# Products that nobody reads, put between TensorE's waits and among the lead's maxima, and one early exponential, in a hybrid block with attention

## What is computed

```
x = x + mix(layernorm(x))          # gate * fuse(causal conv path, symmetric conv path), projections, residual
x = x + ffn(layernorm(x))          # 128 -> 512, relu squared, 512 -> 128, ternary weights and a low-rank part
x = x + attention(layernorm(x))    # 16 heads of size 8
x = x + ffn(layernorm(x))

# attention; B=2 sequences, S=1024 tokens
qkv    = x @ qkv_w.T + qkv_b
scores = q.T k / sqrt(8)
w      = softmax(scores)           # over the keys
out    = (w v) @ out_w.T + out_b
```

## Time and profile before

| | us |
|---|---|
| median of 3 runs | 528.9 (528.67 to 528.9) |
| profiled execution, its own time | 530.41 |
| span of the profiled execution | 528.6 |
| PE busy | 498.6 (94%) |
| DVE busy | 438.3 (83%) |
| ACT busy | 358.3 (68%) |
| POOL busy | 70.2 (13%) |

### The profile page before, as it was taken

The page is one execution under the profiler, slowest core; times in us unless marked ns, Lnnn a source line. Parts: engine busy times, 40 slices in busy tenths (PEclk is TensorE's granted clock), DMA queues, the critical chain, the costliest instruction groups (busy, mean ns, idle before and its releaser), DMA issues.

```text
span 528.6 us, 10281 instructions
## 1 busy us (share of the span) xinstructions
PE 498.6 (94%) x4118; PEld 228.3 (43%) x4118; DVE 438.3 (83%) x654; ACT 358.3 (68%) x691; POOL 70.2 (13%) x89
## 2 busy tenths in 40 slices
PE   4999999998799999999999999999999999998897
PEld 2454566765333333333333333333333333332576
DVE  5699149948897999999999999999999999921953
ACT  2726214354117888888888888888888888888431
POOL 4399930000010001001001000000000000000000
PEclk9999999999757999999999999999999999999899
DMA  8100000053400202003002002101100000000001
GB/s 209 42 2 2 1 9 1 1 208 110 151 10 1 70 15 81 2 2 82 2 1 75 11 1 53 31 1 42 42 2 2 2 2 3 1 1 2 0 21 60
DMA packets 14110, 17.96 MB, mean 34 GB/s; under 512 B 3600, under 2 KB 10175, under 8 KB 13551
## 3 DMA queue, kind: packets, MB, share of 16 engines
q1 hardware_dynamic: 13036, 16.58, 10.7%
q0 software_dynamic: 240, 0.46, 0.5%
q10 hardware_dynamic: 786, 0.27, 0.2%
HBM read 11.70 MB, written 5.24 MB: 32 GB/s over the span
## 4 chain that ended last, share of the span: by engine, by line
PE 82%; DVE 8%; ACT 5%; DMA 2%; issue 1%; SPq 1%; ACTq 0%; DVEq 0%
PE ps L1344 31%; PE ps L1395 26%; PE ps L1137 6%; PE ps L1127 6%; DVE mx L995 4%; PE ps L1148 2%; ACT gate L739 2%; PE ps L1362 2%; PE ps L1173 1%; PE ps L1159 1%; PE ps L1184 1%; PE ps L1114 1%; PE ps L1320 1%; ACT acc L739 1%; DMA x<-in_L_attn_a_x 1%
## 5 line engine op out<-in xcount | busy, mean ns | idle before, releaser
L995 DVE TENSOR_REDUCE mx<-ps 128x1 f32<-128x1024 f32 x256 | 312.8, 1225 | 15.9 <-PE ps L1344 13.8
L1344 PE MATMUL ps<-kt,qt 62*128 62x512 f32 x512 | 195.1, 464 | 7.1 <-DVE mx L995 4.1
L1362 PE MATMUL ps<-qt,kt 64*128 64x512 f32 x512 | 184.3, 452 | 0.8 <-ACT gate L739 0.7
L739 ACT ACTIVATE acc<-ps 128x512 f32<-128x512 f32 x256 | 138.6, 603 | 26.6 <-PE ps L1362 21.8
L739 ACT ACTIVATE gate<-ps 128x512 f32<-128x512 f32 x256 | 138.5, 604 | 15.7 <-PE ps L1362 12.7
L1344 PEld LDWEIGHTS ps<-kt,qt 62*128 62x128 f32 x512 | 80.0, 193 | 110.2 <-DVE mx L995 79.1
L1395 PE MATMUL ps<-gate,val 128*32 128x256 f32 (+1 forms) x976 | 81.4, 405 | 3.8 <-ACT gate L739 3.8
L1395 PE MATMUL ps<-acc,val 128*32 128x256 f32 (+1 forms) x976 | 80.5, 402 | 0.9 <-ACT acc L739 0.9
L1362 PEld LDWEIGHTS ps<-qt,kt 64*128 64x128 f32 x512 | 75.8, 186 | 12.5 <-ACT gate L739 6.4
L498 POOL TENSOR_TENSOR nm_s<-nm,nm_s 16x128 f32<-16x128 f32 x16 | 7.6, 477 | 266.3 <-ACT nm L717 266.3
L1395 PEld LDWEIGHTS ps<-gate,val 128*32 128x32 f32 x976 | 19.3, 108 | 47.2 <-issue 23.5
(11 more groups left out here) (182 smaller groups left out, 369.3 us busy)
## 6 DMA issues: line engine op xcount, KB each, us to landing
qt<-q_scr SPq DMA_DIRECT2D x64, 64.0 KB
kt<-k_scr SPq DMA_DIRECT2D x32, 128.0 KB
x<-in_L_attn_a_x SPq DMA_DIRECT2D x4, 256.0 KB, 5.6
q_scr<-attn SPq DMA_DIRECT2D x4, 256.0 KB, 2.2
k_scr<-attn SPq DMA_DIRECT2D x4, 256.0 KB, 2.4
q_scr<-gate SPq DMA_DIRECT2D x4, 256.0 KB, 2.1
k_scr<-gate SPq DMA_DIRECT2D x4, 256.0 KB, 2.3
qt<-nm_s SPq DMA_DIRECT2D x64, 4.0 KB
```

The costliest lines, as they stand in the source:

```text
L739: act.activation(pexp[step % NPB][:, j, :], bank(e_bank(slot)), ACT.Exp, scale=SCALE).then_inc(e_read, 1)
L995: dve.tensor_reduce(mx[:, item % 2, at:at + 1], pair(lo), AX.X, ALU.max).then_inc(m_read, 1)
L1344: mm = pe.matmul(bank(m_banks(M_UNIT[u])[keys]), qt[r][rows, half, jj, c * P:(c + 1) * P], kt[r][rows, jj, keys, :], start=True, stop=True)
L1362: pe.matmul(bank(e_bank(slot)), kt[r][rows, jj, s // TC, s % TC * P:(s % TC + 1) * P], qt[r][rows, half, jj, :], start=True, stop=True).th ...
```

## The change

A helper `keep_busy(b, n, cols)` on PE issues n float32 products of `ident` with the first `cols` columns of `ident` into PSUM bank b; nothing reads them, they wait for nothing and count no semaphore. Seven of 128 columns stand behind the wait for `ident_ready`, ahead of that for `in_w`, and eight behind the transposes of `in_w`, ahead of the wait for `s_w_fold`; they write bank 5, which nothing uses yet (`IDLE_BANK`). In the lead, two of 96 columns follow each of the units 6 to 21, into bank 2, which is free there. On ACT one exponential of 128x1, of a column of `ident` into a new tile `warm`, stands right behind `negate(0)`.

```
--- before.py
+++ after.py
@@ -60,6 +60,7 @@
 
 EBANKS = (0, 1, 3)
 O_BANK = 2
+IDLE_BANK = 5
 MBANKS = ((4, 5), (6, 7))
 HT = QH * TC
 NU = NI * HT
@@ -254,6 +255,7 @@
         mixed_q = [acc[:, r // 2, 1, r % 2 * CH:(r % 2 + 1) * CH] for r in range(4)]
         mx = sb("mx", [P, 2, HT])
         nm = sb("nm", [HT, P])
+        warm = sb("warm", [P, 1])
         nm_s = sb("nm_s", [HT, PARTS, P])
 
         ps = [ctx.enter_context(nc.psum_tensor(f"ps{i}", [P, 2 * CH], F32)) for i in range(4)]
@@ -723,6 +725,7 @@
                 act.activation(o_sb[:, :], bank(O_BANK), ACT.Copy).then_inc(o_copied, 1)
 
             negate(0)
+            act.activation(warm[:, :], ident[:, 0:1], ACT.Exp)
             for i in range(2):
                 act.wait_ge(scr_done[i], 2 * STORED)
             for hn in range(NI):
@@ -1095,11 +1098,18 @@
         @block.tensor
         def _(pe):
 
+            def keep_busy(b, n, cols):
+
+                for _ in range(n):
+                    pe.matmul(bank(b)[:, 0:cols], ident[:, :], ident[:, 0:cols], start=True, stop=True)
+
             pe.wait_ge(ident_ready, 1)
+            keep_busy(IDLE_BANK, 7, P)
             pe.wait_ge(s_w_in, 16)
             for m in range(4):
                 mm = pe.transpose(bank(1)[:, m * P:(m + 1) * P], in_n[:, m, :], ident[:, :])
             mm.then_inc(setup_mm, 1)
+            keep_busy(IDLE_BANK, 8, P)
             pe.wait_ge(s_w_fold, 16 * 3)
             for i, src in enumerate((hb_n, ha_n)):
                 for k in range(KC):
@@ -1457,6 +1467,7 @@
                 if u == TURN_FIRST_AT:
                     turn_max(0)
                 unit(u)
+                keep_busy(O_BANK, 2, P * 3 // 4)
             for hn in range(NI):
                 n, half = divmod(hn, 2)
                 pe.wait_ge(shift_in, (hn + 1) * SHIFT)
```

## The result

The changed kernel takes 544.04 us in the median of four runs (541.58 to 545.2), against 528.9 for the kernel before: ratio 1.0258, 95% interval 1.0229 to 1.0288. That is 15 us slower. It is the side of the rival *Slower*, for which 538 had been worked out at a chance of 0.05. The profiled execution took 545.2 us with a span of 543.4.

The account below looks back on a forecast made before the run. PE was taken to bound the attention loop, slowed by a low clock. Setup 2.0 plus lead, table and slow half steps 5.2 made 7.2 us off 530.41: 523.2, or 521.7 as the runs' median; range 520.4 to 525.5.

Parts of the forecast that it names:

- Slower: Rival, chance 0.05: lead fillers never raise the clock, each of 15 periods takes 1.98 instead of 1.265 us; total 538.
- Part 1: First loads: setup products raise the clock early, so the run of products starting at 15.96 us comes 2.0 us sooner.
- So it is kept: Setup: the 2.0 us stay won, since evacuations, table load and copy follow from it, then PE works without a break.
- The rule of the Trainium skill weighed there: Setup rival, chance 0.25: transposes neither raise nor hold the clock, so only 0.45 us is gained there; total 523.2.
- Part 2: Lead, units 6 to 21: clock holds, products are hidden, maxima stand 1.14 us apart instead of 1.265; 2.0 us won.
- one fall: Rival, chance 0.15: clock falls at the lead's head, two units at 1.98 us, 1.7 us back; total 523.4 or 524.9.
- The price of a unit's two products: Lead: two 96-column products cost 0.45 us per unit at full clock and 0.85 at the low one.
- the cover that the prediction called thin: Lead at full clock: PE occupied 0.57 + 0.45 = 1.02 of each 1.14 us, products hidden with 0.1 us over.
- the decision point: Lead: the kernel turns slower where the filler at the low clock costs more than 0.14 us per unit.
- Part 3 and the loop's start: Early exponential and attention loop's start: fifth half step's products with v come 5.2 us earlier, lead and table included.
- The table load: ACT's load before the loop's first exponential moves into idle time near 151 us; 1.3 us won.
- The end: Kernel's tail: the clock's fall at 492.8 us may move, vanish or last longer; +-1 us, taken as 0.

Follow-up runs that it names:

- e1: Changed kernel with only the fifteen setup products kept; 529.07 us median of ten, against 530.27 for the kernel before, ratio 0.9987.
- e4: Changed kernel without setup products, plus seven 128-column products ahead of unit 6; 526.15 to 528.15 us in five executions, 532.22, 532.83 and 545.3 in the others.
- e9: e8 plus one product of 512 columns over 64 rows per lead unit; 526.11 us median of ten, ratio 0.9947 to the kernel before.
- e10: e9 plus the fifteen setup products and eight of 128 columns in front of unit 0; 524.13 us median of four, ratio 0.99.
- e11: e10 plus three 128-column products behind the last product with v and five behind the last transpose of o; 524.39 us median of four, ratio 0.9902.
- e3: Changed kernel with only the early exponential kept; 530.44 us median of ten, against 530.27 for the kernel before.
- e7: Changed kernel with each lead unit's two products replaced by one of 512 columns over rows 0 to 63; 524.62 and 542.12 us.
- e12: Changed kernel with sixteen 128-column products behind unit 8 in place of its two of 96; 532.24 us median of eight.
- e8: Kernel before plus the early exponential and seven 128-column products ahead of unit 6; 528.78 us median of ten, against 530.25.

## Why the prediction was wrong

- **Part 1** was right at its own place: the run of products begins at 13.79, where 13.94 had been worked out, and the clock held. From 8.5 to 11.2 us PE did transposes only, with holes, and the next four still took 0.60 us (at 12.23). Two things in it were wrong. "So it is kept" failed in the profiled execution, where 2.17 us were gone at unit 6 by a long issue and a fall that the sum did not have. And 2.0 is the distance to one execution; to the mean of those without setup products it is 1.3 (e1). So that the figure came out is in part luck.
- The rule of the Trainium skill weighed there (TensorE: Matmul & The Clock Gate, Part 4, PE-mode transpose), that transposes do not count as PE work in the way products do, was taken to mean that the clock would fall; in the profiled executions of all eight kernels with setup products it did not. Whether the transposes held it, or it would have stayed up that long without them, was not separated.
- **Part 2, "Will the clock hold here? I take holds": this is the step that failed.** It fell at 137.9 as before, and the mean clocks of the other three runs (0.959 to 0.962) fit a fall at much the same place. The prediction filled the second hole, the one behind unit 6; the first, 1.69 us ahead of it, stayed. With seven products inside that one the clock held in five executions of eight (e4), and in nine of ten and eight of eight with the half-array form (e9; e10 and e11). The hole alone does not settle it: in the eight profiled executions with the hole left open in which the clock fell, it did so between 0.1 us ahead of the start of unit 6 (e3) and 2.9 us behind it (e1), and in e7's it did not fall.
- **The price of that failure was put too low, by a step about coming back.** The rival *one fall* let the clock return after two units, 1.7 us, on the ground that a PE without holes had raised it at 161.8 to 165.2. It had, but with other work: score products in both halves of the array and products with v. In the lead 34.0 us without a hole did not raise it, and 47.4 us with longer products neither; a burst of whole-array products did (e12). "PE busy" in the profile is no sign that the clock will rise. What it is in the lead's work that keeps the clock down stays open. The Trainium skill (TensorE: Matmul & The Clock Gate, Part 1) says that activity releases the throttle; here a PE shown busy all the time did not.
- **The price of a unit's two products was mis-sized at both clocks**: 1.09 us at the low one instead of 0.85, and 0.62 at the full one instead of 0.45. The surplus over four records' pace is 0.25 and 0.18 us; the records' spacing was taken from an unbroken series of one kind, and here PE changes between 62-row and whole-array weights twice per unit. That this change is the surplus was not tested. With 0.66 for the unit itself (taken as 0.57) that makes 1.28 us, so the cover that the prediction called thin was absent: the 2.0 us for the lead was not to be had even with the clock held.
- **The slower rival** had the mechanism and the decision point right: 1.98 us per unit was 2.24. With that figure its total is 15 x 0.98 - 1.3 above 528.9, or 542. From the 530.1 that the kernel before takes in the median of 57 executions, and with 0.8 for the table, it is 544. Its chance of 0.05 was the error. The evidence taken against it was one stretch of different work.
- **Part 3 and the loop's start** were right in kind: 5.0 of 5.2 us in e9. The table load by itself was put too high: it gave 0.8 us instead of 1.3, in the changed kernel and in e3. **The end**: +-1 us taken as 0, and fourteen profiled executions show 0.
- The median that the sum went by came from three runs within 0.3 us, where executions of this kernel lie up to 7 us apart.

## What to carry to other kernels

Put filler work into the hole at which the clock falls, and behind each piece of real work only in a form whose measured pitch still leaves the pacing engine ahead. Here both were needed: the bridge alone won nothing that could be measured (e8), the bridge with half-array products 0.5% (e9). Price it at the low clock too, because there it turns into a loss that holds itself up: the filler makes PE the bound, and need not bring the clock back. And time many executions before a median of three is trusted, and profile more than one: where the clock rises or falls differs from one to the next.

## What the runs showed of the hardware that was not expected

- A TensorE that the profile shows busy for 34.0 us, or for 47.4 us with two records of 512 columns over the whole array among each unit's 62-row products, stayed at 1.2 GHz; a burst of 128-row products, back to back for 6.14 us, brought it to 2.4 GHz 4.8 us after its start. Whether the rows in use, the float32r products or the changes of weights make the difference was not separated. Nor were pauses that the strip of PE cannot show, since the ends of its records are modelled: weight loads stand idle for 0.65 us ahead of each pair of products in the lead.
- Products over rows 0 to 63 with 512 columns cost nothing beside units that alternate between the halves: eleven maxima in 12.54 us. Four records of 96 columns over all rows kept PE for 0.62 us per unit, and the maxima stood 1.27 us apart instead of 1.14.
- Executions of the kernel before, each on one core, differ by up to 7 us (528.1 to 535.4 us). The point of the first rise of the clock is a part of that (14.11 to 16.66 us for the same products, e1), whether and where it falls near 137 another; the fall near the end is none. With the setup products and both bridges eight executions lay within 0.6 us (e10, e11).
